# A state-space scan: copies of its B and C rows stored and read in one transfer each, first loads taken earlier, next rows requested from ScalarE

## The chip, the cores and the metric

The kernel runs on one core of a Trainium2 chip. The metric is the device time of one execution in microseconds (us), lower is better. Each core has TensorE (PE), VectorE (DVE), ScalarE (ACT), GpSimd (POOL) and SyncE (SP); SP and ACT can both request DMA transfers, and the data of all of them is moved by the same 16 DMA engines.

## What is computed

The program is a stack of four layer pairs with layer norms between them, on 2048 tokens of width 1024. The change touches only the selective scan of the third pair (L2 attn). Cut to what matters:

```
proj = hidden_states @ in_proj_w;  x, z = split(proj)          # 2048 channels each
xc   = silu(causal_conv4(x))
ssm_p = xc @ x_proj_w.T  ->  dt_r (64), Bm (16), Cm (16), each rms-normed
dt   = softplus(dt_r @ dt_proj_w.T + dt_bias)                   # per channel and token
A    = -exp(A_log)                                              # per channel and state
for each token t:                                               # 16 states n per channel
    h[d,n] = exp(dt[d]*A[d,n]) * h[d,n] + dt[d]*B_t[n]*x_t[d]
    y[d]   = sum_n h[d,n] * C_t[n]
y = (y + D * xc) * silu(z);   out = y @ out_proj_w.T
```

## The kernel before

Two stages are touched. `l2_inproj` (from L2303) computes xc and ssm_p. Its last work is to store, for each of four chunks of 512 tokens (NT), the 128 rows of ssm (L2357) and, four times over, the 64 rows that hold B and C (L2359). These four copies (COPIES) lie in HBM as `l2_bc`.

`l2_scan` (from L2541) runs over ITEMS = 4 chunks x 16 channel tiles of 128 channels; an item q is one channel tile of one chunk, c is its chunk and ct its tile. An item has NSG = 8 steps of two states each; g numbers the step in the item and st all 512 steps. In each step

- ACT makes dA = exp(dt*A) in a ring of five PSUM banks (L2807),
- POOL makes dBx = dtx*B in one of six slots of `h` (L2838, up to three steps ahead),
- DVE runs the recurrence (L2908, two instructions per step),
- DVE (five steps of eight) or POOL (three of eight) multiplies by C (L2919, L2863),
- PE sums over states with an identity matrix (L2742), and between these does the z projection (L2732) and, from chunk 1 on, the output projection of the chunk before (L2527).

B and C of a chunk stand in `Bb` and `Cb` (128 partitions x 16 states x 512 tokens, the same row in all partitions) and are used by all 16 items of the chunk. They are loaded by state pair: `rows` (L2647) requests, for one pair, four transfers (L2650), each of which takes one copy in HBM and spreads it over a quarter (32) of the partitions. In this document such a set of four, 512 KB in SBUF, is one **group**; a chunk has 16 groups, B0 to B7 and C0 to C7.

All loads and stores stand in one written order on SP. At the start of the scan SP requests ssm, three tables (A, dtb, Dp), the first Wdt and xc, then the 16 groups, with the second Wdt and xc after the fourth, and then Wz. At a chunk's last item (ct = 15) SP first stores y and requests the next xc, Wdt and two loads of the output projection, and then the 16 groups of the next chunk. B(g) waits until POOL has made dBx of that pair in the last item, C(g) until the product with C is done. Each item also takes Wz (512 KB), xc (256 KB), Wdt (64 KB) and the store of y (256 KB), and the output projection takes pieces of oW (128 KB) and oy (512 KB).

Of the kernel before, what the change touches and what calls it, by code (L numbers as in the profile page):

```python
# [15 lines left out]
F32 = mybir.dt.float32  # L16
# [7 lines left out]
P = 128  # L24
D = 1024
# [2286 lines left out]
def l2_inproj(nc, K, w, mem, w_ffn):  # L2312
    xc_dram, ssm_dram = mem.xc, mem.ssm


    with Stage(nc, "l2in") as s:
# [22 lines left out]
        with nc.Block() as block:  # L2339
            @block.sync  # L2340
            def _(e):
                for j in range(2):
                    e.dma_start(W[:, j], w["in_x"][j]).then_inc(w_in[j], 16)
                for dst, name in ((cw, "conv_w"), (cb, "conv_b"), (lnw, "ln_w"), (Wx, "x_proj")):
                    e.dma_start(dst[:], w[name]).then_inc(small_in, 16)
                unpack.index(e)
                for ct in range(CT):
                    if ct % 2 == 0 and ct // 2 < unpack.HT:
                        unpack.load(e, ct // 2)
                    if ct + 2 < CT:  # L2350
# [9 lines left out]
                e.wait_ge(ssm_out, 16 * CHUNKS * (1 + COPIES))  # L2360
                for j in range(2):
                    e.wait_ge(stored[j], 16 * CT // 2)
# [177 lines left out]

def l2_scan(nc, K, w, mem):  # L2541
    xc_dram, ssm_dram, y_dram = mem.xc, mem.ssm, mem.y
# [4 lines left out]
    with Stage(nc, "l2scan") as s:  # L2547
        Bb = s.sb("Bb", [P, NS, NT])
        Cb = s.sb("Cb", [P, NS, NT])
        Wz = s.sb("Wz", [P, 2, KT, P])  # L2550
        Wdt = s.sb("Wdt", [P, 2, P])
        A = s.sb("A", [P, CT, NS])
        dtb = s.sb("dtb", [P, CT])
        Dp = s.sb("Dp", [P, CT])
        carry = s.sb("carry", [P, CT, NS])
        ssm = s.sb("ssm", [P, 2, NT])
        xc = s.sb("xc", [P, 3, NT])
        dt = s.sb("dt", [P, 2, NT])
# [8 lines left out]
        oacc = s.ps("oacc", [P, NT])  # L2567
        small_in = s.sem("small_in")
        a_ok = s.sem("a_ok")
        wz_in = [s.sem(f"wz_in{j}") for j in range(2)]  # L2570
        wdt_in = [s.sem(f"wdt_in{j}") for j in range(2)]
        xc_in = [s.sem(f"xc_in{j}") for j in range(3)]
        ssm_in = [s.sem(f"ssm_in{j}") for j in range(2)]
# [46 lines left out]
        def runs(st):  # L2620
# [3 lines left out]
            return [(slice(j, j + 1), ring[:, (at + j) % BANKS:(at + j) % BANKS + 1, :]) for j in range(SGR)]  # L2624

        with nc.Block() as block:
            @block.sync
            def _(e):
# [17 lines left out]

                def rows(dst, at, c, sem):  # L2647
# [4 lines left out]
                def rows_b(c, g):  # L2652
                    if c:
                        e.wait_ge(dBx_ok, (c * CT - 1) * NSG + g + 1)
                    rows(Bb[:, g * SGR:(g + 1) * SGR, :], B_AT + g * SGR, c, b_in[g])

                def rows_c(c, g):
                    if c:
                        wait_hC(e, (c * CT - 1) * NSG + g)
                    rows(Cb[:, g * SGR:(g + 1) * SGR, :], C_AT + g * SGR, c, c_in[g])  # L2660

                def store(q):
# [4 lines left out]
                low_rank(0)  # L2667
                for dst, name in ((A, "A_log"), (dtb, "dt_bias"), (Dp, "D")):
                    e.dma_start(dst[:], w[name]).then_inc(small_in, 16)
                dt_weights(0)  # L2670
                channels(0)
                for g in range(2):
                    rows_b(0, g)
                    rows_c(0, g)
                dt_weights(1)
                channels(1)
                for g in range(2, NSG):
                    rows_b(0, g)
                    rows_c(0, g)
                z_weights(0)  # L2680
                z_weights(1)
                low_rank(1)
                for q in range(ITEMS):
# [10 lines left out]
                    for n in ahead[:proj.RING]:  # L2694
                        proj.load(e, n)
                    if ct == CT - 1 and c + 1 < CHUNKS:
                        for g in range(NSG):
                            rows_b(c + 1, g)
                            if g >= 2:
                                rows_c(c + 1, g - 2)  # L2700
                        for g in range(NSG - 2, NSG):
                            rows_c(c + 1, g)
                    if q + 2 < ITEMS:
# [62 lines left out]
            def _(a):  # L2766
# [32 lines left out]
                for st in range(STEPS):  # L2799
# [17 lines left out]
            def _(g_):  # L2817
# [27 lines left out]
                for st in range(STEPS):  # L2845
# [10 lines left out]
                    if ct == 0:  # L2856
                        g_.wait_ge(c_in[g], 16 * COPIES * (c + 1))
                    g_.wait_ge(h_ok, st + 1)
# [7 lines left out]
            def _(v):  # L2866
# [26 lines left out]
                for st in range(STEPS):  # L2893
# [16 lines left out]
                    if kind(st) == "Y":  # L2910
# [5 lines left out]
                        if ct == 0:  # L2916
                            v.wait_ge(c_in[g], 16 * COPIES * (c + 1))
                        for js, src in runs(st):
# [382 lines left out]
def build(nc, w, out):  # L3301

    Stage.used = []
    with ExitStack() as ctx:
# [15 lines left out]
        recycle(nc)  # L3320
        l2_inproj(nc, K, w["l2_attn"], l2, w["l2_ffn"])
        l2_scan(nc, K, w["l2_attn"], l2)
        with Stage(nc, "l3first") as s:
# [29 lines left out]
```

## Time and profile before

| | us |
|---|---|
| median of 3 runs | 5386.93 |
| lowest and highest | 5379.96, 5389.9 |
| the profiled execution, its time | 5376.31 |
| the profiled execution, its span | 5374.5 |
| the scan, within that span | 2388.2 to about 4275 |

The span runs from the first to the last instruction; the time is the span and what lies around it, here 1.8 us. A view of windows gives for each stretch the time that each engine was busy, the granted share of PE's full clock, the mean busy share of the 16 DMA engines and what they moved. A timeline row gives start, duration (of all merged instructions together), engine, line and operation, and in brackets how long the engine had been idle and what ended it. `SPq` rows are requests of transfers: their duration is the time on SP, not that of the data.

### The profile page before, as it was taken

The page shows a single profiled execution, that of the slowest core. Times are in us where ns is not written, and L with a number is a line of the kernel's source. Part 1 is how long each engine was busy: PE and PEld are TensorE (multiplying, and loading weights), DVE is VectorE, ACT ScalarE, POOL GpSimd, SP SyncE. Part 2 cuts the span into 40 slices and gives each one's busy share as a digit, 9 for nine tenths or more (in the row PEclk, how much of TensorE's full clock was granted, in tenths as well). Part 3 has the DMA queues.
Part 4 walks back from the last instruction along what each step waited for, and adds up shares of the span by engine and source line. Part 5 has one row for each costly group of instructions (what it writes and reads, how often), then busy time and mean ns, then how long its engine had stood idle before and what let it go on. Part 6 is the DMA issues. An engine that isn't in the chain of part 4 may idle for free. (4 is left out here: it accounts for less than half of the span.)

```text
span 5374.5 us, 40636 instructions
## 1 busy us (share of the span) xinstructions
PE 4917.7 (91%) x14496; PEld 2354.3 (44%) x14496; DVE 3253.8 (61%) x3534; ACT 2119.0 (39%) x2856; POOL 2311.0 (43%) x1219
## 2 busy tenths in 40 slices
PE   8997889989868899968889999999999999999998
PEld 4443234467626444423333444444444344457443
DVE  1663468746457323238999999999999722103522
ACT  1554620045333211126666666666666421102211
POOL 1003430000022100019999999999999742100421
PEclk9898999999979999988989999999999999999999
DMA  2001030000010022142116445444644320000001
GB/s 75 1 1 67 23 126 24 28 16 1 9 34 1 28 70 71 55 107 68 42 34 171 125 135 166 153 136 127 187 136 124 128 82 0 24 0 26 23 16 47
DMA packets 180151, 360.85 MB, mean 67 GB/s; under 512 B 21934, under 2 KB 56878, under 8 KB 175854
## 3 DMA queue, kind: packets, MB, share of 16 engines
q1 hardware_dynamic: 171886, 330.46, 20.1%
q0 software_dynamic: 8064, 27.80, 1.4%
q8 instruction: 116, 1.90, 0.1%
q14 instruction: 85, 0.70, 0.0%
HBM read 300.51 MB, written 57.67 MB: 67 GB/s over the span
## 5 line engine op out<-in xcount | busy, mean ns | idle before, releaser
L2838 POOL TENSOR_TENSOR l2scan_h<-l2scan_dtx,l2scan_Bb 128x1024 f32<-128x1024 f32 x512 | 1199.5, 2361 | 30.3 <-DMA l2scan_Bb<-l_bc 14.8
L2742 PE MATMUL l2scan_yp<-l2scan_h,ident 128*128 128x512 f32 x2048 | 977.2, 611 | 102.8 <-POOL l2scan_h L2863 88.6
L2807 ACT ACTIVATE l2scan_ring<-l2scan_dt,l2scan_A 128x512 f32<-128x512 f32 x1024 | 660.4, 681 | 454.9 <-DVE l2scan_h L2919 352.8
L2742 PEld LDWEIGHTS l2scan_yp<-l2scan_h,ident 128*128 128x128 f32 x2048 | 390.2, 194 | 625.7 <-issue 482.9
L2732 PE MATMUL l2scan_low_z<-state,l2scan_Wz 128*128 128x512 f32 x1024 | 485.5, 607 | 0.3 <-DMA l2scan_Wz<-l_attn_in_z 0.2
L2863 POOL TENSOR_TENSOR l2scan_h<-l2scan_h,l2scan_Cb 128x1024 f32<-128x1024 f32 x192 | 452.7, 2358 | 8.6 <-DVE l2scan_h L2908 0.9
L2401 PE MATMUL l2in_acc<-state,l2in_W 128*128 128x512 f32 x1024 | 444.4, 594 | 11.6 <-DMA l2in_W<-l_attn_in_x 11.6
L2919 DVE TENSOR_TENSOR l2scan_h<-l2scan_ring,l2scan_Cb 128x1024 f32<-128x1024 f32 (+1 forms) x384 | 394.5, 1041 | 6.4 <-DMA l2scan_Cb<-l_bc 1.0
L2908 DVE TENSOR_TENSOR_SCAN l2scan_ring<-l2scan_ring,l2scan_carry,l2scan_h 128x512 f32<-128x512 f32 x320 | 392.7, 1273 | 0.0
L2908 DVE TENSOR_TENSOR_SCAN l2scan_ring<-l2scan_ring,l2scan_h 128x512 f32<-128x512 f32 x320 | 373.3, 1212 | 5.5 <-POOL l2scan_h L2838 5.5
L2527 PE MATMUL l2scan_oacc<-l2scan_oy,l2scan_oW 128*128 128x512 f32 x768 | 353.1, 592 | 0.0
L2732 PEld LDWEIGHTS l2scan_low_z<-state,l2scan_Wz 128*128 128x128 f32 x1024 | 202.0, 197 | 265.2 <-issue 263.4
L2401 PEld LDWEIGHTS l2in_acc<-state,l2in_W 128*128 128x128 f32 x1024 | 194.2, 190 | 259.5 <-issue 247.1
L2456 DVE TENSOR_SCALAR l2in_cv<-l2in_xp,l2in_cw,l2in_cb 128x2048 f32<-128x2048 f32 (+1 forms) x17 | 21.8, 1284 | 395.8 <-ACT l2in_xc L2421 353.4
L2908 DVE TENSOR_TENSOR_SCAN l2scan_h<-l2scan_ring,l2scan_carry,l2scan_h 128x512 f32<-128x512 f32 x192 | 235.2, 1267 | 0.0
L2433 ACT ACTIVATE l2in_xp<-l2in_acc 128x512 f32<-128x512 f32 x64 | 38.3, 598 | 480.9 <-PE l2in_acc L2401 480.9
L2527 PEld LDWEIGHTS l2scan_oacc<-l2scan_oy,l2scan_oW 128*128 128x128 f32 x768 | 145.9, 190 | 183.7 <-issue 183.7
L2188 PE MATMUL l3pair_bank<-state,l3ffn_W 128*128 128x512 f32 x512 | 225.6, 593 | 0.0
L2908 DVE TENSOR_TENSOR_SCAN l2scan_h<-l2scan_ring,l2scan_h 128x512 f32<-128x512 f32 x192 | 223.6, 1207 | 0.4 <-POOL l2scan_h L2838 0.4
L3047 PE MATMUL l2pair_bank<-state,l2ffn_W 128*128 128x512 f32 x512 | 221.6, 592 | 0.0
L710 DVE TENSOR_REDUCE l0att_part<-l0att_SB 128x1 f32<-128x512 f32 x192 | 131.0, 691 | 72.4 <-PE l0att_SB L876 71.9
L147 POOL TENSOR_TENSOR l1proj_part<-state 128x1024 f32<-128x1024 f32 x3 | 7.1, 2351 | 383.3 <-DVE state L1695 383.3
(406 smaller groups left out, 7770.7 us busy)
## 6 DMA issues: line engine op xcount, KB each, us to landing
l2scan_oy<-l_y SPq DMA_DIRECT2D x192, 512.0 KB, 4.9
l2scan_Wz<-l_attn_in_z SPq DMA_DIRECT2D x64, 512.0 KB, 3.5
l2scan_oW<-l_attn_out_w SPq DMA_DIRECT2D x192, 128.0 KB, 3.2
l_xc<-l2in_xc SPq DMA_DIRECT2D x16, 1024.0 KB, 4.8
l2scan_xc<-l_xc SPq DMA_DIRECT2D x64, 256.0 KB, 5.6
l2scan_Bb<-l_bc SPq DMA_DIRECT2D x128, 128.0 KB, 6.9
l2scan_Cb<-l_bc SPq DMA_DIRECT2D x128, 128.0 KB, 7.7
l_y<-l2scan_zs SPq DMA_DIRECT2D x64, 256.0 KB, 5.4
```

The costliest lines, as they stand in the source:

```text
L710: v.tensor_reduce(part[:, H % 2, i // 2, i % 2:i % 2 + 1], SB[:, i % 2, :], AX.X, ALU.max, negate=True).then_inc(max_ok, 1)
L2188: t.matmul(acc, self.W[:, k, m * P:(m + 1) * P], x[:, k, :], start=k == 0, stop=False)
L2401: last = t.matmul(acc[:, n % 4, :], W[:, ct % 2, k, :], x[:, k, :], start=k == 0, stop=k == KT - 1)
L2527: last = t.matmul(self.acc, self.W[:, j, k], self.y[:, j, k], start=kp == 0 and k == 0, stop=kp == PIECES - 1 and k == PIECE - 1)
L2732: last = t.matmul(low_z[:, :], Wz[:, q % 2, k, :], x[:, k, :], start=k == 0, stop=k == KT - 1)
L2742: last = t.matmul(yp[:, :], K.ident[:, :], h[:, st % SLOTS, j, :], start=g == 0 and j == 0, stop=g == NSG - 1 and j == SGR - 1)
L2807: a.activation(bank(st, j), dt[:, q % 2, :], ACT.Exp, scale=A[:, ct, n:n + 1]).then_inc(dA_ok, 1)
L2838: g_.tensor_tensor(h[:, st % SLOTS], dtx[:, None, :].to_broadcast([P, SGR, NT]), Bb[:, g * SGR:(g + 1) * SGR, :], ALU.mult).then_inc(dBx_o ...
L2863: g_.tensor_tensor(hs, hs, Cb[:, g * SGR:(g + 1) * SGR, :], ALU.mult).then_inc(hC_g, 1)
L2908: last = v.tensor_tensor_scan(out, bank(st, j), hs[:, j, :], init, ALU.mult, ALU.add)
L2919: last = v.tensor_tensor(hs[:, js], src, Cb[:, g * SGR + js.start:g * SGR + js.stop, :], ALU.mult)
L3047: last = t.matmul(acc, self.W[:, k, m * P:(m + 1) * P], x[:, k, :], start=k == 0, stop=k == KT - 1)
```

## The change

- `l2_inproj` stores B and C of a chunk with one transfer that writes all four copies (256 rows of 2 KB). In HBM the copies are laid out by chunk, so that the two rows of a pair are one run of 4 KB.
- Tables, both first Wdt and both first xc are held in a stage `l2early` around both stages, and SP requests them in `l2_inproj` after the last store of xc.
- `rows` requests one transfer per group. Its source is written as 4 copies x 32 repetitions x 4 KB, its destination as 128 partitions x 4 KB.
- At the start SP still requests the 16 groups of chunk 0. The groups of later chunks are requested by ACT, between its activations: B(g) after dA of step g of the last item, C(g-3) with it from g = 3, and the last three C groups in the first item of the next chunk.

```
-        self.bc = nc.dram_tensor("l2_bc", (COPIES, P - B_AT, T), F32, kind="Internal").ap()
+        self.bc = nc.dram_tensor("l2_bc", (COPIES, CHUNKS, P - B_AT, NT), F32, kind="Internal").ap()
...
+                early.load(e)
+                for j in range(2):
+                    e.wait_ge(stored[j], 16 * CT // 2 - 16)
+                early.channels(e)
...
-                    for r in range(COPIES):
-                        e.dma_start(mem.bc[r][:, i * NT:(i + 1) * NT], sq[B_AT:P, i, :]).then_inc(ssm_out, 16)
+                    e.dma_start(mem.bc[:, i].rearrange("r p t -> p r t"),
+                                sq[B_AT:P, i, None, :].to_broadcast([P - B_AT, COPIES, NT])).then_inc(ssm_out, 16)
...
-                    for r in range(COPIES):
-                        src = mem.bc[r][at - B_AT:at - B_AT + SGR, c * NT:(c + 1) * NT]
-                        e.dma_start(dst[r * SHARE:(r + 1) * SHARE], src[None, :, :].to_broadcast([SHARE, SGR, NT])).then_inc(sem, 16)
+            src = mem.bc[:, c, at - B_AT:at - B_AT + SGR, :].rearrange("r g t -> r (g t)")
+            e.dma_start(dst.rearrange("p g t -> p (g t)"), src[:, None, :].to_broadcast([COPIES, SHARE, SGR * NT])).then_inc(sem, 16)
...
+                    if ct == CT - 1 and c + 1 < CHUNKS:
+                        rows_b(a, c + 1, g)
+                        if g >= 3:
+                            rows_c(a, c + 1, g - 3)
+                    if ct == 0 and c and g < 3:
+                        rows_c(a, c, g + NSG - 3)
...
-                        g_.wait_ge(b_in[g], 16 * COPIES * (q // CT + 1))
+                        g_.wait_ge(b_in[g], 16 * (q // CT + 1))
```

On SP, at the start of the scan, there stood (tile names are those of the code with the stage's name ahead; the numbers behind are shapes, and x4 is four alike):

```order
L2645 DMA l2scan_ssm<-l_ssm 128x512
L2669 DMA l2scan_A<-l_attn_A_log 128x256
L2669 DMA l2scan_dtb<-l_attn_dt_bias 128x16
L2669 DMA l2scan_Dp<-l_attn_D 128x16
L2638 DMA l2scan_Wdt<-l_attn_dt_proj 128x128
L2642 DMA l2scan_xc<-l_xc 128x512
L2650 DMA l2scan_Bb<-l_bc 32x2x512 x4
L2650 DMA l2scan_Cb<-l_bc 32x2x512 x4
L2650 DMA l2scan_Bb<-l_bc 32x2x512 x4
```

and in the changed kernel, at the same place:

```order
L2682 DMA l2scan_ssm<-l_ssm 128x512
L2651 DMA l2scan_Bb<-l_bc 128x1x1024
L2651 DMA l2scan_Cb<-l_bc 128x1x1024
L2651 DMA l2scan_Bb<-l_bc 128x1x1024
L2651 DMA l2scan_Cb<-l_bc 128x1x1024
L2651 DMA l2scan_Bb<-l_bc 128x1x1024
```

The five small loads have gone ahead of this place, and each group is one row.

On SP, at the last item of chunk 0, the groups of chunk 1 stood between two loads of the output projection and the next Wz:

```order
L2516 DMA l2scan_oW<-l_attn_out_w 128x256
L2517 DMA l2scan_oy<-l_y 128x2x512
L2650 DMA l2scan_Bb<-l_bc 32x2x512 x12
L2650 DMA l2scan_Cb<-l_bc 32x2x512 x4
L2650 DMA l2scan_Bb<-l_bc 32x2x512 x4
```

They now stand on ACT, in the same item, between its activations; the first of them there are

```order
L2816 ACTIVATE l2scan_ring<-l2scan_dt,l2early_A 128x512 x8
L2651 DMA l2scan_Bb<-l_bc 128x1x1024
L2816 ACTIVATE l2scan_ring<-l2scan_dt,l2early_A 128x512 x2
L2651 DMA l2scan_Bb<-l_bc 128x1x1024
L2803 ACT_TABLE_LOAD
L2803 ACTIVATE l2scan_zs<-l2scan_low_z 128x512
L2816 ACT_TABLE_LOAD
L2816 ACTIVATE l2scan_ring<-l2scan_dt,l2early_A 128x512 x2
L2651 DMA l2scan_Bb<-l_bc 128x1x1024
L2816 ACTIVATE l2scan_ring<-l2scan_dt,l2early_A 128x512 x2
L2651 DMA l2scan_Bb<-l_bc 128x1x1024
L2651 DMA l2scan_Cb<-l_bc 128x1x1024
```

Nothing moves on PE, DVE and POOL.

## Rows read from the trace of the kernel before

**Rows 1.** The page: span; queue; costliest group (busy, mean | idle); requests, us to landing.
```profile
span 5374.5 us, 40636 instructions
...
q1 hardware_dynamic: 171886, 330.46, 20.1%
...
L2838 POOL TENSOR_TENSOR l2scan_h<-l2scan_dtx,l2scan_Bb 128x1024 f32<-128x1024 f32 x512 | 1199.5, 2361 | 30.3 <-DMA l2scan_Bb<-l_bc 14.8
...
l2scan_Bb<-l_bc SPq DMA_DIRECT2D x128, 128.0 KB, 6.9
l2scan_Cb<-l_bc SPq DMA_DIRECT2D x128, 128.0 KB, 7.7
```

**Rows 2.** Windows of the scan, by chunk: busy time of each engine, clock, DMA share, GB/s.
```profile
2402.40:2870.00 467.60, 380.31 (x768) 155.32 (x769) 427.57 (x502) 301.76 (x412) 452.41 (x253) 0.89 0.24 59
2870.00:3340.00 470.00, 467.15 (x1085) 205.71 (x1084) 459.82 (x439) 312.36 (x424) 460.27 (x216) 1.00 0.51 151
```

**Rows 3.** SP's timeline from the stores to the scan's first groups.
```profile
2373.46 0.32 SPq L2357 DMA_DIRECT2D l_ssm<-l2in_sq  x1
2373.83 2.41 SPq L2359 DMA_DIRECT2D l_bc<-l2in_sq  x4
...
2383.03 2.55 SPq L2359 DMA_DIRECT2D l_bc<-l2in_sq  x4
2388.23 0.32 SPq L2645 DMA_DIRECT2D l2scan_ssm<-l_ssm  x1
...
2390.01 0.43 SPq L2638 DMA_DIRECT2D l2scan_Wdt<-l_attn_dt_proj  x1
2390.49 0.43 SPq L2642 DMA_DIRECT2D l2scan_xc<-l_xc  x1
2390.96 1.84 SPq L2650 DMA_DIRECT2D l2scan_Bb<-l_bc  x4
```

**Rows 4.** Windows: 4 KB rows to 128 partitions; the stores; groups of chunk 0.
```profile
1819.00:1820.00 1.00, 0.12 (x1) 0.12 (x1) 0.00 (x0) 0.00 (x0) 0.00 (x0) 0.50 1.02 414
2374.00:2386.00 12.00, 0.00 (x0) 0.00 (x0) 1.41 (x3) 0.12 (x1) 0.00 (x0) 0.50 0.88 242
2402.00:2422.00 20.00, 5.60 (x7) 1.77 (x7) 15.09 (x19) 14.35 (x21) 14.62 (x9) 0.59 1.07 226
```

**Rows 5.** DMA view of 1573 to 1576.9: two transfers of 128 rows.
```profile
DMA packets 288, 0.04 MB, mean 9 GB/s; under 512 B 288, under 2 KB 288, under 8 KB 288
```

**Rows 6.** DMA view of 1576.9 to 1577.6: one transfer of 8 rows of 4 KB.
```profile
DMA packets 16, 0.03 MB, mean 47 GB/s; under 512 B 8, under 2 KB 8, under 8 KB 16
```

**Rows 7.** PE, POOL and DVE in the first item (timelines).
```profile
2392.25 2.07 PE L2722 MATMUL l2scan_low_z<-l2scan_ssm,l2scan_Wdt 128*128 128x512 f32 x2 [22.41 <-DMA l2scan_Wdt<-l_attn_dt_proj]
...
2402.45 4.65 POOL L2838 TENSOR_TENSOR l2scan_h<-l2scan_dtx,l2scan_Bb 128x1024 f32<-128x1024 f32 x2
...
2441.09 1.28 DVE L2919 TENSOR_TENSOR l2scan_h<-l2scan_ring,l2scan_Cb 128x512 f32<-128x512 f32 x2
```

**Rows 8.** Timelines, chunk 0 to 1: ACT at step 0 of ct 15; DVE, first use of C7.
```profile
2845.39 1.30 ACT L2807 ACTIVATE l2scan_ring<-l2scan_dt,l2scan_A 128x512 f32<-128x512 f32 x2 [2.26 <-DVE l2scan_h L2919]
...
2907.02 1.23 DVE L2919 TENSOR_TENSOR l2scan_h<-l2scan_ring,l2scan_Cb 128x1024 f32<-128x1024 f32 x1
```

**Rows 9.** The same two rows for chunk 2 to 3.
```profile
3773.16 1.30 ACT L2807 ACTIVATE l2scan_ring<-l2scan_dt,l2scan_A 128x512 f32<-128x512 f32 x2 [2.26 <-DVE l2scan_h L2919]
...
3835.79 1.23 DVE L2919 TENSOR_TENSOR l2scan_h<-l2scan_ring,l2scan_Cb 128x1024 f32<-128x1024 f32 x1
```

**Rows 10.** Tile Wz: us from its request to its landing.
```profile
DMA to landing us min/median/max: 3.2/3.5/12.6
```

**Rows 11.** SP at chunk 0 to 1: y, output projection, first and last groups, Wz.
```profile
2856.60 0.33 SPq L2665 DMA_DIRECT2D l_y<-l2scan_zs  x1
...
2859.88 6.80 SPq L2650 DMA_DIRECT2D l2scan_Bb<-l_bc  x12
...
2885.87 5.59 SPq L2650 DMA_DIRECT2D l2scan_Cb<-l_bc  x12
2891.50 0.42 SPq L2632 DMA_DIRECT2D l2scan_Wz<-l_attn_in_z  x1
```

More of the change, by code:

```diff
@@ L2306, in __init__, with load, channels, l2_inproj @@
         self.ssm = nc.dram_tensor("l2_ssm", (P, T), F32, kind="Internal").ap()
-        self.bc = nc.dram_tensor("l2_bc", (COPIES, P - B_AT, T), F32, kind="Internal").ap()
+        self.bc = nc.dram_tensor("l2_bc", (COPIES, CHUNKS, P - B_AT, NT), F32, kind="Internal").ap()
         self.y = nc.dram_tensor("l2_y", (CT, P, T), F32, kind="Internal").ap()
         self.rows = nc.dram_tensor("l2_rows", (D, D), F32, kind="Internal").ap()
-def l2_inproj(nc, K, w, mem, w_ffn):
+class ScanFirst:
+    def __init__(self, s, w, mem):
+        self.w, self.mem = w, mem
+        self.A = s.sb("A", [P, CT, NS])
+        self.dtb = s.sb("dtb", [P, CT])
+        self.Dp = s.sb("Dp", [P, CT])
+        self.Wdt = s.sb("Wdt", [P, 2, P])
+        self.xc = s.sb("xc", [P, 3, NT])
+        self.small_in = s.sem("small_in")
+        self.wdt_in = [s.sem(f"wdt_in{j}") for j in range(2)]
+        self.xc_in = [s.sem(f"xc_in{j}") for j in range(3)]
+    def load(self, e):
+        for dst, name in ((self.A, "A_log"), (self.dtb, "dt_bias"), (self.Dp, "D")):
+            e.dma_start(dst[:], self.w[name]).then_inc(self.small_in, 16)
+        for q in range(2):
+            e.dma_start(self.Wdt[:, q, :], self.w["dt_proj"][:, q * P:(q + 1) * P]).then_inc(self.wdt_in[q], 16)
+    def channels(self, e):
+        for q in range(2):
+            e.dma_start(self.xc[:, q, :], self.mem.xc[q][:, 0:NT]).then_inc(self.xc_in[q], 16)
+def l2_inproj(nc, K, w, mem, w_ffn, early):
     xc_dram, ssm_dram = mem.xc, mem.ssm
@@ L2538, in add, with l2_scan @@
         v.tensor_tensor(x, self.acc, x, ALU.add).then_inc(self.added, 1)
-def l2_scan(nc, K, w, mem):
+def l2_scan(nc, K, w, mem, early):
     xc_dram, ssm_dram, y_dram = mem.xc, mem.ssm, mem.y
@@ L2550, in l2_scan @@
         Wz = s.sb("Wz", [P, 2, KT, P])
[L2551 to L2554, printed above, removed]
+        Wdt, A, dtb, Dp, xc = early.Wdt, early.A, early.dtb, early.Dp, early.xc
         carry = s.sb("carry", [P, CT, NS])
         ssm = s.sb("ssm", [P, 2, NT])
-        xc = s.sb("xc", [P, 3, NT])
         dt = s.sb("dt", [P, 2, NT])
@@ L2567, in l2_scan @@
         oacc = s.ps("oacc", [P, NT])
-        small_in = s.sem("small_in")
+        small_in, wdt_in, xc_in = early.small_in, early.wdt_in, early.xc_in
         a_ok = s.sem("a_ok")
         wz_in = [s.sem(f"wz_in{j}") for j in range(2)]
-        wdt_in = [s.sem(f"wdt_in{j}") for j in range(2)]
-        xc_in = [s.sem(f"xc_in{j}") for j in range(3)]
         ssm_in = [s.sem(f"ssm_in{j}") for j in range(2)]
@@ L2624, in runs, with rows, rows_b, rows_c @@
             return [(slice(j, j + 1), ring[:, (at + j) % BANKS:(at + j) % BANKS + 1, :]) for j in range(SGR)]
+        def rows(e, dst, at, c, sem):
+            src = mem.bc[:, c, at - B_AT:at - B_AT + SGR, :].rearrange("r g t -> r (g t)")
+            e.dma_start(dst.rearrange("p g t -> p (g t)"), src[:, None, :].to_broadcast([COPIES, SHARE, SGR * NT])).then_inc(sem, 16)
+        def rows_b(e, c, g):
+            if c:
+                e.wait_ge(dBx_ok, (c * CT - 1) * NSG + g + 1)
+            rows(e, Bb[:, g * SGR:(g + 1) * SGR, :], B_AT + g * SGR, c, b_in[g])
+        def rows_c(e, c, g):
+            if c:
+                wait_hC(e, (c * CT - 1) * NSG + g)
+            rows(e, Cb[:, g * SGR:(g + 1) * SGR, :], C_AT + g * SGR, c, c_in[g])
         with nc.Block() as block:
@@ L2667, in _ @@
                 low_rank(0)
[L2668 to L2671, printed above, removed]
                 for g in range(2):
[L2673 to L2676, printed above, removed]
+                    rows_b(e, 0, g)
+                    rows_c(e, 0, g)
                 for g in range(2, NSG):
-                    rows_b(0, g)
-                    rows_c(0, g)
+                    rows_b(e, 0, g)
+                    rows_c(e, 0, g)
                 z_weights(0)
@@ L2695, in _ @@
                         proj.load(e, n)
[L2696 to L2702, printed above, removed]
                     if q + 2 < ITEMS:
@@ L2856, in _ @@
                     if ct == 0:
-                        g_.wait_ge(c_in[g], 16 * COPIES * (c + 1))
+                        g_.wait_ge(c_in[g], 16 * (c + 1))
                     g_.wait_ge(h_ok, st + 1)
@@ L2916, in _ @@
                         if ct == 0:
-                            v.wait_ge(c_in[g], 16 * COPIES * (c + 1))
+                            v.wait_ge(c_in[g], 16 * (c + 1))
                         for js, src in runs(st):
@@ L3320, in build @@
         recycle(nc)
-        l2_inproj(nc, K, w["l2_attn"], l2, w["l2_ffn"])
-        l2_scan(nc, K, w["l2_attn"], l2)
+        with Stage(nc, "l2early") as s:
+            early = ScanFirst(s, w["l2_attn"], l2)
+            l2_inproj(nc, K, w["l2_attn"], l2, w["l2_ffn"], early)
+            l2_scan(nc, K, w["l2_attn"], l2, early)
         with Stage(nc, "l3first") as s:
```

11 lines of the change are left out of this document (1 added, 10 removed).

## The prediction, made before the changed kernel was run

> **What bounds the kernel now.** I read the page first, then the scan by windows, then the timelines at the places where groups of B and C are loaded. In the scan four engines take turns as the bound: in chunk 0 POOL is busy 452.4 of 467.6 us, in chunk 1 PE is busy 467.2 and POOL 460.3 of 470 us [rows 2]. So the scan has next to no slack: a stall in it is not made up for later. What the change can win is small and stands in one row of the page: over the whole scan POOL waited 14.8 us for groups of B [rows 1]. What it can lose is larger, since every item of a chunk needs all 16 groups of that chunk, and a late group stops POOL or DVE, and soon all.
>
> **The stores.** SP goes from 16 requests of B and C to 4. Before, the first store was requested at 2373.5, the last block ended at 2385.6 and the scan began at 2388.2 [rows 3]. But the requests were hardly what took the time: in this stretch the DMA engines were busy 0.88 of it and moved 242 GB/s [rows 4]. The bytes stay the same, 4 x (256 KB + 4 x 128 KB) = 3.1 MB, and 3.1 MB at 242 GB/s is 13 us, from 2374 to 2387. I take a gain of 0.5 us; the bounds are 0 and, if the rate rose to the 414 GB/s of the best window [rows 4], 3.1 MB in 7.6 us, a gain of 5 us.
>
> The row that holds this is the 242 GB/s. The Trainium skill, SBUF — State Buffer, section Door 1, says that partitions 64 to 127 reach only 8 of 16 ports at 27.2 GB/s each, 218 GB/s; B and C stand in just those partitions, and the trace agrees (242 GB/s, with the ssm stores on all partitions among it).
>
> **The small loads.** Five requests go ahead of the scan (0.47 us each, from 2388.60 to 2390.96 [rows 3]). In `l2_inproj` they stand behind the last store of xc, when SP waits for the norm, so they cost nothing there; if that cover were gone they would cost their 2.3 us. The first matmul of the scan waited for Wdt until 2392.25, 4.0 us after the scan's first request [rows 7]; with Wdt there it waits for ssm, which lands after some 2.3 us, a gain of 1.7 us. It counts only if the groups aren't what ends the first item.
>
> **The groups: how many DMA engines carry one.** Before, a group was four transfers, each written as 32 repetitions, and chunk 0's groups went at 226 GB/s with all 16 engines busy [rows 4]: 512 KB in 2.3 us. Now the source of one transfer is written with 4 copies outermost. How a transfer is shared among the engines shows in the counts of packets, since each engine that takes part adds one small packet at the end. Two transfers of 128 rows left 288 packets, 256 of data and 32 others, 16 for each transfer [rows 5]; one transfer of 8 rows of 4 KB left 16, 8 of data and 8 others [rows 6]. So one with 8 outermost ran on 8 engines. A source with 4 outermost and a destination with 128 isn't in the trace; if the share is made on whole outermost entries of both, it is 4 engines, each with 32 runs of 4 KB. I take 4.
>
> The Trainium skill says it outright: DMA: Bandwidth & Descriptors, section Why a DMA increments its semaphore by 16 and not by 1, has the number of engines as the largest up to 16 that divides the slowest dimension of both sides, and its Rules for kernel authors warn of a leading broadcast of c copies, which confines the whole DMA to c engines. By it the sum is the one below; without it, that of the first rival.
>
> **What a group then takes.** 128 KB pass through each of the four engines. One engine's rate has three rows: 414/16 = 25.9 GB/s (4 KB rows spread over all partitions), 226/16 = 14.1 GB/s (each transfer in one quarter of the partitions) [rows 4], and the mean of the whole execution, 330.46 MB in 20.1% of 16 x 5374.5 us, 19.1 GB/s [rows 1]. The new transfer is like the first in its 4 KB runs and like the second in that each engine may walk one quarter. I take the mean: 131,072 B / 19.1 = 6.9 us a group, with 5.1 and 9.3 us as the ends. All groups go through the same four engines, so a chunk's 16 take 110 us (81 and 149), where the trace had 16 x 2.3 = 37 us.
>
> **Start of the scan.** The 16 groups are requested in a row and C7 is last. Request plus first data is 0.4 + 1.9 us (Wz, 32 KB per engine or 1.3 us of data, landed after 3.2 us at the least [rows 10]). C7 lands at 2.3 + 110 = 112.7 us after the scan's first request. Before, DVE first used C7 at 2441.1, which is 52.9 us after 2388.2 [rows 3, 7]. So the first item ends 60 us later (31 and 98). Wz comes right behind C7 in SP's order, 1.3 us later, and is hidden by it. Less the 0.5 us of the stores: +59 us.
>
> **The three changes of chunk.** ACT asks for B0 after dA of step 0 of ct 15. In chunk 0 that ended at 2845.4 + 1.3 = 2846.7, and DVE first used C7 at 2907.0, 60.3 us later [rows 8]; at the last change it is 61.3 us [rows 9]. B0's data starts at 2849.0, and from then on four engines always have groups queued, since ACT asks for one or two a step (470 us / 128 steps = 3.7 us [rows 2]), faster than they are carried. C7 is there after 110 us more, plus what SP's queue puts through the same engines meanwhile: two items at 1088 KB (y, xc, Wdt, Wz) and five pieces of the output projection at 640 KB, 5376 KB or 344 kB per engine, 18 us at 19.1 GB/s. So C7 lands at 2849 + 110 + 18 = 2977, 70 us late. I take off 3 us for what runs ahead (POOL three steps, ACT two and a half): 67 us (34 with 5.1 us a group and 13 us of SP's, 112 with 9.3 and 24), three times: 201 us (102 and 336).
>
> ACT's own cost is small: 16 requests of 0.43 us [rows 3] per chunk, 7 us, in items where ACT is busy 312 of 470 us [rows 2]; and C5 is asked for behind a wait for POOL's product of step 5, ahead of dA of the next step; dA itself had waited 2.26 us for DVE to free its bank [rows 8], which covers a short wait. SP, rid of the groups, asks for Wz some 30 us earlier (2859.9 against 2891.5 [rows 11]), which helps nobody while groups are late.
>
> **Sum.** 59 + 201 = +260 us; on the profiled execution's 5376 us that is 5636. The median of the three runs stands 10.6 us above that execution, so the forecast is 5647 us. The ends: 5376 - 0.5 + 31 + 102 = 5509 and 5376 - 0.5 + 98 + 336 = 5810, with the 10.6 us 5519 and 5820.
>
> **Rivals.**
>
> *All 16 engines carry a group (0.17).* For it: the destination has 128 partitions outermost, and nothing in the trace shows a transfer whose two sides differ. Then one transfer spreads over all partitions with 4 KB runs, at between 226 and 414 GB/s, 1.3 to 2.3 us a group. POOL's 14.8 us of waits go, the stores give 0.5 and Wdt up to 1.7 us; some of the 14.8 comes back as other waits. I take -15 us: 5372 us against 5387. This is the one that ends on the other side. The point from which it decides: at 3.3 us a group C7 lands at 2849 + 53 + 5 (SP's part) = 2907, just when DVE wants it, so any transfer that takes less is hidden at the changes of chunk.
>
> *Four engines, each undisturbed, 5.1 us a group (0.25):* 5519 us, the lower end above. Against it speaks that the same rows by quarters ran at 14.1 GB/s an engine.
>
> *Four engines that hinder each other in pairs, 9.3 us a group (0.23):* 5820 us. For it speaks that same row; against it, that there 16 engines wrote one quarter of the partitions, and here one does.
>
> *Requests that hold up ACT.* If ACT can't hand over a request while nine groups are queued, dA comes late too. It would overlap the same stall and move the time by less than the ends above differ; it is in them.
>
> **How the numbers follow.** My forecast, four engines at about 6.9 us, has 0.35, the two ends 0.25 and 0.23, 16 engines 0.17. The range from 5490 to 5830 us holds the three cases of four engines with 20 us to spare below and leaves out the fourth. A difference of 0.2%, 11 us, is about what a measurement of this kernel can tell from none. Of the 0.17 I give 0.11 to faster and 0.05 to the same, since -15 us is only just beyond 11; slower gets 0.84.
>
> **What would show it.** In the profile after: ACT and SP requests of Bb and Cb each with a median to landing of tens of us, rising through a chunk to 60 us and more, where before it was 6.9 and 7.7 [rows 1]; POOL's and DVE's waits for DMA of Bb and Cb of some 200 us in total instead of 14.8; the DMA share low (near 4/16) and the rate 60 to 105 GB/s in the first 80 us of the scan; the scan's first request still near 2388; and the items between the changes of chunk as long as before. If instead the groups land in under 5 us, it was 16 engines and the whole of the forecast falls.

## The result and the profile after

| | before | after |
|---|---|---|
| median, us | 5383.44 (4 runs, 5375.6 to 5389.9) | 5556.97 (4 runs, 5556.18 to 5560.11) |
| span of the profiled execution | 5374.5 | 5554.4 |

The changed kernel takes 1.0329 times the time of before (95% interval 1.0316 to 1.0342), 173.5 us more by the medians and 179.9 by the two spans. Slower, inside the range, but 90 us short of the forecast.

From the page of the changed kernel: span, requests from SP (q1) and from ACT (q10), and the costliest groups of the scan (busy, mean | idle before them and what ended it). They answer to [rows 1].

```profile
span 5554.4 us, 40437 instructions
...
q1 hardware_dynamic: 153326, 305.28, 17.5%
...
q10 hardware_dynamic: 6336, 25.17, 1.2%
...
L2853 POOL TENSOR_TENSOR l2scan_h<-l2scan_dtx,l2scan_Bb 128x1024 f32<-128x1024 f32 x512 | 1197.8, 2358 | 80.9 <-DMA l2scan_Bb<-l_bc 47.0
...
L2878 POOL TENSOR_TENSOR l2scan_h<-l2scan_h,l2scan_Cb 128x1024 f32<-128x1024 f32 x192 | 452.1, 2355 | 73.2 <-DVE l2scan_h L2923 65.6
...
L2934 DVE TENSOR_TENSOR l2scan_h<-l2scan_ring,l2scan_Cb 128x1024 f32<-128x1024 f32 (+1 forms) x384 | 394.5, 1041 | 39.4 <-DMA l2scan_Cb<-l_bc 33.8
L2923 DVE TENSOR_TENSOR_SCAN l2scan_ring<-l2scan_ring,l2scan_carry,l2scan_h 128x512 f32<-128x512 f32 x320 | 392.8, 1273 | 27.9 <-ACT l2scan_ring L2816 27.9
L2923 DVE TENSOR_TENSOR_SCAN l2scan_ring<-l2scan_ring,l2scan_h 128x512 f32<-128x512 f32 x320 | 373.5, 1213 | 57.2 <-ACT l2scan_ring L2816 35.2
```

The instructions of POOL and DVE are no slower (POOL's dBx 2358 ns against 2361), and PE's sum over states is so by 1% (617 ns against 611). The time is in waits: 47.0 us of POOL for B, 33.8 of DVE for C, and 63.1 of DVE for dA from ACT. POOL's 65.6 us for DVE's recurrence are waits of DVE seen once more.

**How many engines carry a group.** The DMA view of the changed kernel from 2392 to 2450, while nothing but groups of chunk 0 is carried; it answers to the third row of [rows 4]:

```profile
DMA packets 1501, 5.97 MB, mean 103 GB/s; under 512 B 44, under 2 KB 44, under 8 KB 1501
...
q1 hardware_dynamic: 1501, 5.97, 25.6%
```

Two readings say four. The share of 16 engines is 25.6%, and the 1457 packets of data are 11.4 groups of 128, so that the 44 small packets are four to a group, in the way in which [rows 5, 6] gave 16 and 8. A group takes 512 KB at 103 GB/s, 5.1 us; an engine moves 25.7 GB/s. The rule of the Trainium skill weighed in the prediction (DMA: Bandwidth & Descriptors, Why a DMA increments its semaphore by 16 and not by 1) says four here, and the trace agrees.

**The first item.** SP's timeline of the changed kernel, from the scan's first request:

```profile
2386.38 0.32 SPq L2682 DMA_DIRECT2D l2scan_ssm<-l_ssm  x1
2386.75 0.62 SPq L2651 DMA_DIRECT2D l2scan_Bb<-l_bc  x1
2387.42 0.52 SPq L2651 DMA_DIRECT2D l2scan_Cb<-l_bc  x1
2387.99 0.51 SPq L2651 DMA_DIRECT2D l2scan_Bb<-l_bc  x1
2388.53 3.65 SPq L2651 DMA_DIRECT2D l2scan_Cb<-l_bc  x1
2392.23 0.51 SPq L2651 DMA_DIRECT2D l2scan_Bb<-l_bc  x1
2392.78 10.61 SPq L2651 DMA_DIRECT2D l2scan_Cb<-l_bc  x1
2403.43 5.03 SPq L2651 DMA_DIRECT2D l2scan_Bb<-l_bc  x1
...
2449.19 4.88 SPq L2651 DMA_DIRECT2D l2scan_Cb<-l_bc  x1
2454.11 5.97 SPq L2669 DMA_DIRECT2D l2scan_Wz<-l_attn_in_z  x2
```

From the fourth group on SP is held until the engines have carried one: most requests take 4.9 to 5.0 us, and one that takes 0.5 is followed by one of over 10. So Wz is requested only at 2454.1. POOL's dBx with B7, DVE's first use of C7 and, behind it, the z projection on PE (three timelines; they answer to [rows 7]):

```profile
2470.93 2.34 POOL L2853 TENSOR_TENSOR l2scan_h<-l2scan_dtx,l2scan_Bb 128x1024 f32<-128x1024 f32 x1 [7.27 <-DMA l2scan_Bb<-l_bc]
...
2475.97 1.29 DVE L2934 TENSOR_TENSOR l2scan_h<-l2scan_ring,l2scan_Cb 128x512 f32<-128x512 f32 x2
...
2477.25 4.78 PE L2741 MATMUL l2scan_low_z<-state,l2scan_Wz 128*128 128x512 f32 x6 [10.97 <-DMA l2scan_Wz<-l_attn_in_z]
```

C7 is used 89.6 us after the first request, where it was 52.9: 36.7 us late. The wait that the trace shows ahead of it is not for C7 but for B7, the group before it: POOL stood 7.27 us for B7 until 2470.93, the recurrence on DVE followed, and DVE then took C7 without a wait. All of POOL's 47.0 us for B lie in this first item. PE had waited 10.97 us for Wz when its z projection began, 1.3 us after the first use of C7.

**The changes of chunk.** ACT at the end of chunk 0 in the changed kernel (timeline; ACTq rows are its requests, and "issue" in brackets is time in which ACT waited for nothing but itself), and DVE's first use of C7 of chunk 1. They answer to [rows 8]:

```profile
2887.91 1.10 ACTq L2651 DMA_DIRECT2D l2scan_Bb<-l_bc  x1
...
2902.84 5.50 ACTq L2651 DMA_DIRECT2D l2scan_Bb<-l_bc  x1
2908.38 7.05 ACTq L2651 DMA_DIRECT2D l2scan_Cb<-l_bc  x1
2915.48 0.63 ACT L2791 ACTIVATE l2scan_u<-l2scan_u 128x512 f32<-128x512 f32 x1 [11.95 <-issue]
...
2922.18 10.96 ACTq L2651 DMA_DIRECT2D l2scan_Bb<-l_bc  x1
...
2933.18 6.90 ACTq L2651 DMA_DIRECT2D l2scan_Cb<-l_bc  x1
2940.13 0.69 ACT L2816 ACTIVATE l2scan_ring<-l2scan_dt,l2early_A 128x512 f32<-128x512 f32 x1 [16.71 <-issue]
...
2995.18 1.22 DVE L2934 TENSOR_TENSOR l2scan_h<-l2scan_ring,l2scan_Cb 128x1024 f32<-128x1024 f32 x1 [4.78 <-DMA l2scan_Cb<-l_bc]
```

The requests stop ACT as they stop SP, and dA is late with them. From B0's request to C7's first use it is 107.3 us, where it was 60.3.

**Where the 180 us lie.** POOL's dt*x (L2828 before, L2843 after) marks the items. From the scan's first request to the third item's mark it is 121.0 us against 75.4, +45.6. Over the four items around each change it is 162.6, 167.9 and 164.8 us against 118.5, 121.2 and 121.3: +44.1, +46.7, +43.5, +134.3 together. The items between keep their 28.3 and 29.0 us. With a start of the scan that lay 1.9 us earlier in this execution this makes 178.0 of the 179.9 us.

### The profile page after: what moved, and what is told of

The parts are those of the page before. It is cut to its first block and busy times, and to the rows that moved or that the text cites. A ratio compares the mean times of both kernels' runs of the same rounds, so it can differ in the third digit from the quotient of the medians.

```text
span 5554.4 us, 40437 instructions
## 1 busy us (share of the span) xinstructions
PE 4940.7 (89%) x14496; PEld 2358.2 (42%) x14496; DVE 3255.0 (59%) x3534; ACT 2120.0 (38%) x2856; POOL 2309.3 (42%) x1219
## 5 line engine op out<-in xcount | busy, mean ns | idle before, releaser
L2853 POOL TENSOR_TENSOR l2scan_h<-l2scan_dtx,l2scan_Bb 128x1024 f32<-128x1024 f32 x512 | 1197.8, 2358 | 80.9 <-DMA l2scan_Bb<-l_bc 47.0
L2751 PE MATMUL l2scan_yp<-l2scan_h,ident 128*128 128x512 f32 x2048 | 990.7, 617 | 194.3 <-POOL l2scan_h L2878 123.6
L2816 ACT ACTIVATE l2scan_ring<-l2scan_dt,l2early_A 128x512 f32<-128x512 f32 x1024 | 661.2, 681 | 599.7 <-DVE l2scan_h L2934 402.6
L2878 POOL TENSOR_TENSOR l2scan_h<-l2scan_h,l2scan_Cb 128x1024 f32<-128x1024 f32 x192 | 452.1, 2355 | 73.2 <-DVE l2scan_h L2923 65.6
L2934 DVE TENSOR_TENSOR l2scan_h<-l2scan_ring,l2scan_Cb 128x1024 f32<-128x1024 f32 (+1 forms) x384 | 394.5, 1041 | 39.4 <-DMA l2scan_Cb<-l_bc 33.8
L2836 POOL TENSOR_TENSOR l2scan_l<-l2scan_l,l2scan_dt 128x512 f32<-128x512 f32 x64 | 81.3, 1270 | 232.4 <-ACT l2scan_l L2797 232.2
```

Source lines behind the costliest of these rows:

```text
L2751: last = t.matmul(yp[:, :], K.ident[:, :], h[:, st % SLOTS, j, :], start=g == 0 and j == 0, stop=g == NSG - 1 and j == SGR - 1)
L2853: g_.tensor_tensor(h[:, st % SLOTS], dtx[:, None, :].to_broadcast([P, SGR, NT]), Bb[:, g * SGR:(g + 1) * SGR, :], ALU.mult).then_inc(dBx_o ...
L2878: g_.tensor_tensor(hs, hs, Cb[:, g * SGR:(g + 1) * SGR, :], ALU.mult).then_inc(hC_g, 1)
L2934: last = v.tensor_tensor(hs[:, js], src, Cb[:, g * SGR + js.start:g * SGR + js.stop, :], ALU.mult)
```

## Experiments

Every edit is to the changed kernel. Times are medians; each ratio is to the kernel before on the same chip (5379.58 us beside the first four kernels, 5381.96 beside the next four, 5383.25 beside the last two).

**e1: the repetitions outermost.** The same one transfer with the same rows; only the order in which the source is written differs. Partition p now reads copy p mod 4.

```
-  src[:, None, :].to_broadcast([COPIES, SHARE, SGR * NT])
+  src[None, :, :].to_broadcast([SHARE, COPIES, SGR * NT])
```

> The changed kernel with the source of each group written as 32 repetitions outermost and the 4 copies inside them, where it was 4 copies outermost and 32 repetitions inside. Bytes, copies, requests, waits and destination are the same; partition p now reads copy p mod 4. Theory (the number of outermost entries of the source sets how many DMA engines carry a group): 16 engines, a group in 1.3 to 2.3 us, POOL's and DVE's waits for Bb and Cb under 15 us together, 5360 to 5375 us. Rival 1 (runs of 4 KB read over and over from few places in HBM are slow, whichever engines read them): stays near 5557. Rival 2 (the stall comes from ACT's waits and requests, the engines matter little): most of the loss stays, 5450 or more.

Measured: 5363.16 us, ratio 0.9969 (0.9957 to 0.9982). DMA view of 2394 to 2410:

```profile
DMA packets 1796, 6.53 MB, mean 408 GB/s; under 512 B 198, under 2 KB 198, under 8 KB 1796
...
q1 hardware_dynamic: 1796, 6.53, 102.0%
```

1598 packets of data are 12.5 groups, and 198/12.5 is 16 small ones to a group: all 16 engines. This one line of order is worth 194 us and turns the loss into a gain of 16 by the medians. The marks of the items say the same: 7.2 us are gained by the third item's mark and 9.5 at the three changes of chunk. POOL's wait for B has gone from the page:

```profile
L2853 POOL TENSOR_TENSOR l2scan_h<-l2scan_dtx,l2scan_Bb 128x1024 f32<-128x1024 f32 x512 | 1196.9, 2357 | 14.1 <-PE l2scan_yp L2751 7.5
```

**e2: four transfers to a group, as before, with runs of 4 KB and the new requests.**

```
+  for r in range(COPIES):
+      src = mem.bc[r, c, at - B_AT:at - B_AT + SGR, :].rearrange("g t -> (g t)")
+      e.dma_start(dst[r * SHARE:(r + 1) * SHARE].rearrange("p g t -> p (g t)"), src[None, :].to_broadcast([SHARE, SGR * NT])).then_inc(sem, 16)
```

> The changed kernel with each group again as four transfers, one copy to one quarter of the partitions each, from the new layout (runs of 4 KB), requested from ACT where the change put them. Theory: each transfer has 32 entries outermost, so 16 engines; but a quarter of the partitions takes 2.3 us a group as before. 64 requests of 0.43 us per chunk stand on ACT, 27 us in some 10 steps. 5365 to 5395 us. Rival 1 (slow source): near 5557. Rival 2 (requests on ACT): slower than before by more than 50 us.

Measured: 5369.08 us, ratio 0.9976 (0.9966 to 0.9985). Here the groups went at 227 GB/s (DMA view of 2394 to 2410), as before [rows 4] in spite of the longer runs. So the loss is not in the layout in HBM, the earlier small loads or the place of the requests, but in the one transfer.

**e3: four engines, all groups requested from SP**, at a chunk's last item behind y, xc, Wdt and the pieces of the output projection, as before the change (`e` is SP, `a` ACT).

```
+                    if ct == CT - 1 and c + 1 < CHUNKS:
+                        for g in range(NSG):
+                            rows_b(e, c + 1, g)
+                            if g >= 2:
+                                rows_c(e, c + 1, g - 2)
...
-                    if ct == CT - 1 and c + 1 < CHUNKS:
-                        rows_b(a, c + 1, g)
-                        if g >= 3:
-                            rows_c(a, c + 1, g - 3)
```

> The changed kernel (4 copies outermost, so four engines) with the groups of later chunks requested from SP, at the last item, as before the change. ACT has no requests. Theory: a group still takes 5.1 us and a queue takes about four such transfers before the requester is held up; now SP is held up in place of ACT, and with it Wz, xc and the output projection's loads that stand behind. First item unchanged (+43 us against before), each change of chunk +35 to +50 us (measured with ACT: +44 to +47): 5530 to 5580. Rival 2 (what costs is that ACT is held up and dA comes late): each change of chunk only +10 to +20 us, 5450 to 5490.

Measured: 5555.4 us, ratio 1.0323 (1.0305 to 1.034), the same as with ACT. The page shows the waits in their plain form:

```profile
L2854 POOL TENSOR_TENSOR l2scan_h<-l2scan_dtx,l2scan_Bb 128x1024 f32<-128x1024 f32 x512 | 1198.1, 2358 | 180.3 <-DMA l2scan_Bb<-l_bc 162.8
...
L2935 DVE TENSOR_TENSOR l2scan_h<-l2scan_ring,l2scan_Cb 128x1024 f32<-128x1024 f32 (+1 forms) x384 | 394.3, 1041 | 149.4 <-DMA l2scan_Cb<-l_bc 144.1
```

ACT isn't stopped any more, and POOL and DVE wait for the groups themselves, 162.8 and 144.1 us (largely the same stall seen from two engines). Over the same four items the changes are +43.6, +41.4 and +42.5 us here, 127.5 together, against 134.3 with ACT's requests (134.3 in e7 and 138.6 in e8 too, which have them). So the held requests on ACT are in the main a way in which the late groups show; some 7 us are more than that, by one traced execution of each kernel. The medians can't show them, since the moment at which the scan begins moves by more than that (12.7 us later here than in the changed kernel's execution). The page of the changed kernel has one wait that this one lacks, of the output projection on PE for its load oy from SP:

```profile
L2556 PE MATMUL l2scan_oacc<-l2scan_oy,l2scan_oW 128*128 128x512 f32 x768 | 360.0, 602 | 10.3 <-DMA l2scan_oy<-l_y 10.3
```

It is two waits, 5.4 us at the second change and 4.8 at the third. With the groups on ACT's queue, oy is requested and carried beside them; with all on SP it stands in one order with them.

**e4: e1's source, all groups requested from SP.** The edits of e1 and e3 together.

> Both edits: source with 32 repetitions outermost, and the groups of later chunks requested from SP. Theory: as the first of these runs within 10 us, since with 16 engines neither queue is held up; what ACT's requests are worth by themselves shows as the difference, which I expect at 0 to 8 us in favour of ACT: 5365 to 5380. Rival 2: clearly faster than the first run, by 20 us or more.

Measured: 5362.99 us, ratio 0.9965 (0.9952 to 0.9977), against 5363.16 with ACT's requests. With 16 engines that part of the change is worth nothing that can be measured (the three changes of chunk take 351.5 us in e1 and 351.1 here); with 4 it costs the 7 us of e3. The time is 2 us below the range expected.

**e5: all partitions read copy 0.** Four copies are still stored, 128 repetitions of one run of 4 KB are read. The rival was that 16 engines hinder each other on one run.

```
-  src[:, None, :].to_broadcast([COPIES, SHARE, SGR * NT])
+  src[0:1, :].to_broadcast([P, SGR * NT])
```

> The changed kernel with every group read from the first copy alone, its source written as 128 repetitions of one 4 KB run; four copies are still stored. Theory (outermost entries set the engines): 16 engines. What it tells beyond the swap: whether the copies matter. If 16 engines reading one 4 KB run are as quick as with four, 5360 to 5370 us and some 410 GB/s in the first item; if they hinder each other as the loads of the weight scales did before the change (one 4 KB row to 64 partitions, 135 to 160 GB/s), a group takes 3.3 us or more, the first item is 0 to 10 us longer than with the swap, 5370 to 5385 us. If the copies, and not the engines, were what made the changed kernel slow (rival 1), it stays above 5500.

Measured: 5356.25 us, ratio 0.9955 (0.9938 to 0.9971). DMA view of 2378 to 2390 in 40 slices, GB/s in each:

```profile
GB/s 102 287 321 314 369 246 123 178 218 178 150 246 273 328 287 355 355 410 437 423 341 410 382 410 410 410 423 423 437 423 423 437 396 423 437 410 396 410 396 423
```

Once the small loads of the start are through, one run feeds all partitions at 396 to 437 GB/s, against 408 in e1. No hindrance; the copies aren't needed for the loads. The time is 4 us below the range expected. The 135 to 160 GB/s that the expectation gives for the weight scales are single slices of a view; over 1825.5 to 1827.5, while they are carried, the mean is 213.

**e6: eight copies, the copies outermost.** It puts a group on 8 engines and tests the point that the prediction set for the first rival (under 3.3 us a group the changes of chunk hide it).

```
-COPIES = 4
+COPIES = 8
```

> The changed kernel with 8 copies stored and 8 outermost in the source (16 repetitions inside). Theory: 8 engines, so 26 GB/s x 8 = 207 GB/s and 2.5 us a group, under the 3.3 us at which a group is just in time: nothing is late at the changes of chunk, and the first item is as before. The stores grow from 3.1 to 5.2 MB, at 242 GB/s 8.7 us more ahead of the scan. 5368 to 5380 us. If the loss grew in proportion to the time of a group (no threshold), it would keep about half of 178 us, 5470. The request queue: with 17 packets per engine and transfer in place of 33, a requester is held up only behind some 7 transfers if the limit is in packets, still behind 4 if it is in transfers.

Measured: 5416.12 us, ratio 1.0059 (1.0036 to 1.0081), slower than expected. Windows of the store phase, then the DMA view of 2410 to 2440:

```profile
2380.22:2404.97 24.75, 0.00 (x0) 0.00 (x0) 1.95 (x3) 0.66 (x2) 0.00 (x0) 0.50 0.89 212
```

```profile
DMA packets 1599, 6.18 MB, mean 206 GB/s; under 512 B 90, under 2 KB 90, under 8 KB 1599
...
q1 hardware_dynamic: 1599, 6.18, 54.0%
```

Eight engines, 2.5 us a group. The store phase is 10.0 us longer than before's 14.8, and the first item, between the marks of POOL, 3.8 us (37.4 against 33.6). The rest that belongs to the scan is at the changes of chunk (+6.0, +7.9 and +4.7 us over the same four items as above), though a group takes less than 3.3 us. The page has waits that e1 lacks:

```profile
L2853 POOL TENSOR_TENSOR l2scan_h<-l2scan_dtx,l2scan_Bb 128x1024 f32<-128x1024 f32 x512 | 1198.3, 2359 | 44.6 <-PE l2scan_yp L2751 27.4 <-DMA l2scan_Bb<-l_bc 10.9
...
L2556 PE MATMUL l2scan_oacc<-l2scan_oy,l2scan_oW 128*128 128x512 f32 x768 | 356.9, 597 | 17.0 <-DMA l2scan_oy<-l_y 17.0
```

The views of waits place them. POOL's 10.9 us for B are all in the first item. At the second and third change PE waited 9.7 and 7.4 us for oy, the load of the output projection from SP, and DVE only 0.4 and 2.0 us for C; at the first, ahead of which no output projection runs, DVE waited 5.3 us for C. So the point of 3.3 us was reckoned from the last group alone, and what came late at two of the three changes was another load. That oy is late because it shares the engines with the groups is my reading: with groups on 16 engines (e1) and with all on SP (e3) the wait is absent.

**e7: four engines, Wz requested ahead of the groups** (its first two pieces, before chunk 0's groups).

```
+                z_weights(0)
+                z_weights(1)
...
-                z_weights(0)
-                z_weights(1)
```

> The changed kernel (four engines) with the two first Wz requested ahead of the 16 groups of chunk 0 instead of behind them. In the changed kernel PE waited 11 us for Wz in the first item and the second item was 5 us longer than usual. Theory: Wz at the end of a held-up queue is part of the first item's loss: 5 to 9 us faster than the changed kernel, 5545 to 5555 us; the changes of chunk stay as they are. If the groups alone set the first item, no difference.

Measured: 5553.81 us, ratio 1.0325 (1.0307 to 1.0343), 3 us less than the changed kernel: less than was expected, and within what the measurement can tell. The traces tell it apart a little: from C7's first use to the third item's mark it is 22.5 us before, 31.4 in the changed kernel and 26.8 here, so the late Wz cost 4.6 us; some 1.5 of them are lost again because C7 itself comes 91.1 instead of 89.6 us after the first request. The other 4.3 of the 8.9 us remain with Wz early.

**e8: chunk 0 on 16 engines, chunks 1 to 3 on four** (e1's source for c = 0 only).

```
+  src = src[:, None, :].to_broadcast([COPIES, SHARE, SGR * NT]) if c else src[None, :, :].to_broadcast([SHARE, COPIES, SGR * NT])
```

> The changed kernel with the swap (16 engines) for the groups of chunk 0 alone; those of chunks 1 to 3 keep 4 copies outermost. Theory: the first item's loss goes (43 us, and the 7 us that it now gains), the three changes of chunk keep their 44 to 47 us each and lose what they gained (5 us): 5357 + 3 x 48 = 5500 to 5515 us. If one late chunk drags the others (or they overlap), the two parts don't add up.

Measured: 5502.21 us, ratio 1.0224 (1.0205 to 1.0243). It is 54.8 us below the changed kernel and 139 above e1: the start of the scan is worth the first (45.6 us lost, and the 7.2 that e1 gains there), the three changes the second. In the traces the third item's mark comes 68.0 us after the scan's first request (68.1 in e1), and the three changes cost 138.6 us against before, where they cost 134.3 in the changed kernel. The parts add up within 5 us.

**e9: one copy and two copies, the repetitions outermost.**

```
-COPIES = 4
+COPIES = 1
...
-  src[:, None, :].to_broadcast([COPIES, SHARE, SGR * NT])
+  src[None, :, :].to_broadcast([SHARE, COPIES, SGR * NT])
```

> One copy of B and C instead of four, stored and read, and the 128 repetitions of a group are the outermost entries of its source, so that all 16 engines should carry it. The stores shrink from 3.1 MB to 1.6 MB (four times 256 KB of ssm and 128 KB of B and C). My theory is that the store phase goes by bytes through the ports of the upper partitions: at some 210 to 240 GB/s it takes 7 to 8 us in place of 14.7, and the groups go at about 410 GB/s as they did with all groups read from copy 0. That gives 5357 to 5363 less 6 to 7 us, so about 5346 to 5357, ratio 0.993 to 0.996. Rival: the scan's start is set by something else that ends beside the stores (the last normed rows, a semaphore), then the phase shrinks by under 2 us and the time stays at 5356 to 5363. Second rival: the ssm stores alone are what the phase waits for; then the same.

> Two copies, stored and read, with the 64 repetitions outermost in a group's source. By the theory of bytes the stores are 2.1 MB and the phase takes 9 to 10 us in place of 14.7; the groups at about 410 GB/s. That gives about 5350 to 5359. Rival: no change against four copies, 5356 to 5363. If one copy is the fastest and two lie between it and four, each copy costs its bytes (some 2.2 us for each 512 KB); if the two don't differ, the stores were not what the time went by.

Measured: one copy 5353.71 us, ratio 0.9944 (0.9931 to 0.9957); two copies 5359.65 us, ratio 0.9949 (0.9935 to 0.9962). Windows from the first store to the scan's first request, for one copy, then for two, then for the changed kernel with four:

```profile
2370.66:2377.86 7.20, 0.00 (x0) 0.00 (x0) 1.94 (x3) 0.65 (x2) 0.00 (x0) 0.52 0.71 219
```

```profile
2376.90:2386.45 9.55, 0.00 (x0) 0.00 (x0) 1.95 (x3) 0.65 (x2) 0.00 (x0) 0.51 0.80 220
```

```profile
2371.70:2386.40 14.70, 0.00 (x0) 0.00 (x0) 1.96 (x3) 0.66 (x2) 0.00 (x0) 0.51 0.85 214
```

The phase goes by bytes, as the theory had it: 7.2, 9.55, 14.7 and, with eight copies, 24.75 us at 219, 220, 214 and 212 GB/s. The phases of one and of two copies fell where they were expected; by the whole time one copy did too, and two came out 0.65 us above theirs. Whether one copy also beats four by the whole time stays open: the intervals of e1, e5 and both kernels here touch or overlap, since the phase begins anywhere from 2361.6 to 2376.9 in these executions, though all that is ahead of it is the same program. One copy is the fastest version by its median and the simplest.

## Why the prediction came out as it did

*What bounds the kernel: right.* A stall in the scan is not made up for; items beside the stalls keep their length, and e8 shows the stalls adding up.

*The stores: right.* The forecast was 0.5 us, it was 0.1 (14.77 us before, from the first store to the scan's first request [rows 3], 14.67 after), though SP's requests fell from 20 to 8. e9 and e6 confirm the reason, that the bytes set it: the rate stays at 212 to 220 GB/s for one to eight copies. A further copy of B and C, 0.52 MB, took 2.35 us from one to two copies, 2.56 each from two to four and 2.52 each from four to eight, which is 205 to 223 GB/s. The Trainium skill (SBUF — State Buffer, Door 1) counts eight ports for partitions 64 to 127, where B and C stand, and 218 GB/s for eight ports. The traces agree with that number, but no run stored them from other partitions, so it is not shown that the ports set it.

*The small loads: right, at 0.* The groups ended the first item. The 1.7 us on offer were not there either: with Wdt loaded early, PE's first matmul waited for ssm and began 4.7 us after the scan's first request (4.0 in e1), where it was 4.0 before.

*Four engines: right.* Shown by the packets and the 25.6%, and by e1, where the order of the source alone gives 16. The first rival was the wrong mechanism for this kernel, but its price was good: -15 us forecast for 16 engines, -16 in e1.

*A group in 6.9 us: the step that was mis-sized.* It took 5.1. I had taken the mean of the whole execution, 19.1 GB/s an engine, because the new transfer resembled both the 25.9 and the 14.1 GB/s rows. It behaved as the first. The four quarters at 14.1 are slow with four transfers (e2, 227 GB/s again with runs of 4 KB), not because one engine writes one quarter of the partitions: if the split is on whole outermost entries, one engine does just that in the changed kernel, at 25.7. The mean of an execution in which many small packets are carried was no estimate of this transfer. So the "four undisturbed" case held for the rate (its time of 5519 did not), and "hinder each other in pairs" fell.

*The start of the scan: 59 forecast, 45.6 measured, 31 at the low end.* C7 was used 36.7 us late, 5.7 later than 16 groups of 5.1 us and the 2.3 ahead of them make. POOL's two last waits for B ended at 2457.56 and 2470.93, 13.4 us for two groups where 10.2 were due, while Wz, ssm and xc were requested and carried beside them; what delayed them was not separated. "Wz comes right behind C7, 1.3 us later" fits (PE began at 2477.25), "and is hidden by it" failed: PE had stood still 10.97 us for it, the whole z projection of the item was still to do, and together with what else had piled up this added 8.9 us (45.6 - 36.7). e7 assigns 4.6 of it to Wz; for the rest I have no experiment. PE's granted clock was 0.52 until 2476, near the lower of its two levels (1.2 GHz), and whether that matters was not separated.

*The changes of chunk: 67 each forecast, 44.8 on average, 34 at the low end.* The path was right: from B0's request to C7's use less the 60.3 us of before less some 3 us ahead, 107.3 - 60.3 - 3 = 44, and it was 44.1. (The row at 2845.39 [rows 8] merges the last dA of step 0 with the first of step 1, so the mark that corresponds to B0's request at 2887.91 is 2845.4 and not 2846.7; with it the 60.3 are 61.6 and the 44 are 43.) The low end was too low because SP's transfers share the engines less cheaply than I had it. DMA view of the changed kernel from 2890 to 2995:

```profile
DMA packets 5478, 14.39 MB, mean 137 GB/s; under 512 B 368, under 2 KB 1264, under 8 KB 5476
...
q10 hardware_dynamic: 2100, 8.34, 21.3%
q1 hardware_dynamic: 3376, 6.03, 20.4%
```

The groups (q10) took 21.3% of 16 x 105 us, on four engines 89 us for 16 groups, 5.6 us each beside other traffic. SP's 6.03 MB took 20.4%, 21 us of every engine at 17.6 GB/s, where the low end had 13 us. 89 + 21 = 110 us, with a little overlap the 107 seen. For mixed traffic a rate near the mean, 19.1, was the better one; for the groups alone it was the wrong one. The sum had no term for the output projection's own loads coming late, on which PE waited 5.4 and 4.8 us at two of the changes (e3).

*"Requests that hold up ACT": right that it comes, and nearly right that it overlaps the late groups.* I thought of nine groups in the queue; it began with the fourth on SP and the fifth on ACT. e3 takes ACT's requests away, and some 7 us of the 134 at the changes go with them.

*The deciding point of 3.3 us: wrong.* With 2.5 us a group (e6) the changes still cost 18.7 us, in part by the wait for oy and not for groups.

*The sum.* 260 forecast, 179.9 in the two spans. Against 5.1 us a group and my own path the rest is +14.6 at the start (8.9 behind C7 and the 5.7) and +11 at each change (SP's share, and groups at 5.6 us). These are two errors of opposite sign: the dearer group put the forecast 128 us above the low end, and some 47 us around the groups were missing. The range was wide enough for both; with the right 5.1 us a group my sum gave 5519, 38 us too low.

## What to carry to other kernels

Before merging several transfers into one, ask which entry is outermost on each side: a leading count of 4 put a group on 4 of 16 engines, and the same bytes with a leading 32 on all 16. Two numbers of the DMA view tell it at once, the queue's share (25.6% while it is the only one with work) and the small packets for each transfer. Price a confined transfer by a row of the same size of run at an undisturbed engine, and what it shares engines with by a mixed one; look which other loads of the same stage are on those engines, since one of them may be the last wait; and put nothing behind a long queue that another engine needs.

## What the runs showed of the hardware that was not expected

- The queue holds the engine that requests. With 33 packets per engine and transfer (32 runs and one small) the fourth group's request took 3.65 us and most later ones 4.9 to 10.6; with 17 per engine (e6) the first six took 0.57 to 0.93 us and the seventh 2.29; with 9 no group's request at the start took over 0.72 (e1) and 1.35 (e5), though at 0.65 us a request and 1.3 us a group some eight groups then waited at once (an estimate). So it goes by packets rather than by transfers; where the limit lies was not measured. On ACT this stopped activations up to 16.7 us.
- 16 engines can read one and the same run of 4 KB at 396 to 437 GB/s (e5).
- Four transfers, each to a quarter of the partitions, went at 226 to 227 GB/s with all 16 engines busy, with rows of 2 KB (before, [rows 4]) and of 4 KB (e2) alike; one transfer over all partitions at 408. Why, no run here tells.
- A request of B on ACT took 327 ns (median) when its source was one run with 128 repetitions (e5) and 521 ns with 32 repetitions of four copies (e1).
